# Twelve late turns, an earlier first step: reordering the middle stage of a two-layer gated cross-attention kernel

## The chip, the cores and the metric

One Trainium2 (trn2) chip, one of its cores. The metric is the device time of one execution in microseconds (us), median of the timed runs. The engines of the core are named as the profile names them: PE (TensorE, matrix products), PEld (its weight loads), DVE (VectorE), ACT (ScalarE), POOL (GpSimd) and SP (SyncE, which issues DMAs).

## The reference

Two layers over `x` of 4 batches x 512 rows x 512 columns, with a context of 4 x 512 x 256:

```python
# layer 0, per batch: attention over the context's 512 rows, which mixes the 512 columns of x
query, key = ctx @ Wq.T + bq, ctx @ Wk.T + bk                      # 512 x 128
attention = softmax(query @ key.T)                                 # 512 x 512
x = x + tanh(g_xattn[0]) * (layernorm(x) @ attention.T)
weight = einsum('oin,n->oi', sigmoid(pweight) - sigmoid(nweight), exps * sigmoid(mask)) * scale
x = x + tanh(g_ffn[0]) * (layernorm(x) @ weight.T + bias)          # bias from 4 bits as well
# layer 1: cross-attention, 16 heads of 128, then 16 experts of which each row takes 4
q, k, v = rmsnorm(layernorm(x) @ Wq), rmsnorm(ctx @ Wk), ctx @ Wv
x = x + tanh(g_xattn[1]) * (softmax(q @ k.T / sqrt(128)) @ v @ Wo)
x = x + tanh(g_ffn[1]) * experts(layernorm(x), topk_idx, topk_weight)
```

What matters below: layer 1's queries need a normalised and transposed copy of `x` for every batch, and the experts need a routing table that is made from `topk_idx` alone. In this problem only batch 0 goes through the experts.

## The kernel before, in words

**Numbers in two parts.** Every product of two fp32 matrices is made of three PE products (`product`): each operand is held as a rounded high part and the low rest, and `lo*hi`, `hi*hi`, `hi*lo` are summed in one PSUM bank. The high part is a copy on ACT (`copy_hi`, L824), the low one a subtraction on DVE (`lower`, L1153) or POOL (L1661).

**Stage 0 (layer 0).** Each engine runs a list of two-character entries written by hand: `L0_ORDER` for PE, `ACT_ORDER`, `DVE_ORDER`, `POOL_ORDER`, and `LOAD_ORDER` for SP. The letters: `K` splits of the context and of Wq/Wk, `Q` the two small projections of batch b, `R` the bias turned into a row, `S` and `T` the energies and the softmax, `P` the turned probabilities, `G` and `W` the sixteen bit planes and the four slices of the weight made of them, `C0` to `C15` the sixteen row tiles of the first wide product (attention times x), `E0` to `E15` those of the second (normalised x times weight, 12 products of 512 columns each), `m`/`C`/`E` on POOL the layer norms, `d` and `D` the normalised rows of batch b (ACT) and their turns (PE transposes, ACT high, DVE low), `B` the bias added. `f` and `F` are the same as `d` and `D` after the second wide product: they make `xnT`, the operand of layer 1's queries, for batches 0 to 3. A turn is four transposes of 128x128 into one PSUM bank. `Y` and `Z` on DVE work out the bit weights and the bias.

**Stage 1 (layer 1's attention) and the experts.** `step(t)` runs for t = 0 to 65. A step is a software pipeline three deep: the projections of item t (`key_value`, `query`), the scores and probabilities of item u = t-1, the values and output product of item w = t-2. Items 0 to 15 are the 16 heads of batch 0; the items from 16 on are, head by head, batches 1, 2 and 3. From step 20 the experts' work is packed in beside it. Before, steps 0 and 1 stand at the end of the hand-written lists: `X0` is step 0 (`key_value`, `ranks`, `query`), `x0` its key turn on PE, `X1` step 1. The routing table runs inside them: `experts()` and `slots()` (DVE) and `ranks()` (PE) in step 0, `places()` (DVE `x0`) after it, `tokens_in`, `spot` (DVE) and `table()` (PE) in step 1.

**What ties step 0 to stage 0.** `ranks` writes both `w_bank`s, which the wide products use, so it waits for the last of them. The high and low parts of layer 0's weight (`wf`) live in the tensors `kv` that hold keys and values of a step, so no step's keys can be written before E15. A step's scores wait for `q_lo` and `kT_lo`, both made by DVE in its own list order:

```python
if i == 0:
    need(pe, q_lo, 1, u, 1)
    need(pe, kT_lo, 1, u, 1)
```

Of the kernel before, what the change touches and what calls it, by code (L numbers as in the profile page):

```python
# [12 lines left out]
P = 128  # L13
# [29 lines left out]
def stages(text):  # L43
# [16 lines left out]
    E0 E1 E2 E3 D2 E4 E5 E6 E7 D3 E8 E9 F1 E10 E11 F0 E12 E13 F2 E14 E15 X0 x0 F3 X1""")  # L60
ACT_ORDER = stages("""
    K0 K1 K2 Q0 G0 R0 K3 S0 T0 A0 Q1 A1 P0 A2 A3 S1 K4 A4 A5 G1 T1 P1 K5 A6 Q2 A7 G2 d0 A8 G3 S2 A9 G4 W0 G5 A10 T2
    G6 G7 P2 Q3 A11 A12 A13 G8 W1 d1 G9 G10 S3 D0 G11 T3 G12 W2 P3 G13 A14 G14 G15 A15 W3 D1 d2 D2 d3 D3 f1 F1 f0 F0
    H0 f2 F2 X0 f3 x0 F3 z0 X1""")
DVE_ORDER = stages("""
    Y0 K0 K1 K2 Z0 Q0 R0 S0 G0 T0 m0 Q1 P0 S1 m1 C0 C1 T1 C2 C3 P1 G1 Q2 m2 G2 S2 C4 G3 C5 T2 G4 C6 G5 C7 G6 P2 G7
    Q3 m3 G8 C8 S3 G9 C9 G10 T3 G11 D0 P3 G12 C10 G13 C11 G14 C12 G15 C13 C14 C15 E0 E1 D1 E2 E3 D2 E4 E5 E6 E7 D3
    E8 E9 F1 E10 E11 F0 E12 E13 F2 E14 E15 X0 F3 x0 X1""")
POOL_ORDER = stages("""
    G0 K3 A0 A1 A2 m0 K4 A3 A4 m1 A5 G1 C0 G2 K5 A6 m2 G3 A7 G4 W0 A8 G5 A9 G6 A10 G7 C1 G8 W1 G9 A11 G10 A12 G11  # L70
    A13 G12 W2 G13 A14 G14 m3 G15 A15 W3 C2 B0 B1 C3 B2 E0 B3 E1 E2 H0 E3 X0 X1""")

LOAD_ORDER = stages("""
    c0 c1 g0 c2 x0 t0 x1 c3 t1 g1 c4 g2 x2 g3 t2 g4 g5 g6 g7 g8 t3 g9 x3 g10 g11 g12 g13 g14 g15""")
# [16 lines left out]
EARLY_TURNS, _ = numbered("DFPR", L0_ORDER[:L0_ORDER.index(("X", 0))])  # L91
EARLY = max(n + (1 if key[0] == "R" else NT) for key, n in EARLY_TURNS.items())
# [10 lines left out]
P_BANK = (1, 0, 1, 1)  # L103
LAST_SCORES = NI
# [19 lines left out]
def flamingo_kernel(nc, x, xT, ctxT, vecs, w0, bits, w1, w_gu, w_dn, topk_idx, topk_w, x0_dram, rows_dram, y_dram, out):  # L124
# [3 lines left out]
    with ExitStack() as ctx:  # L128
# [117 lines left out]
        def turn_bank(n):  # L246

            return (t_bank + j_bank)[n % 4] if n < EARLY else (s_bank + t_bank[1:] + j_bank[:1])[(n - EARLY) % 4]

# [4 lines left out]
        def prob_bank(t, i):  # L254

            return (t_bank[1], t_bank[0], s_bank[1], j_bank[1])[i] if t == LAST_SCORES else t_bank[P_BANK[i]]

# [8 lines left out]
        def energy_bank(b, i):  # L266
# [40 lines left out]
            sem("s_mm"), sem("s_max"), sem("p_exp"), sem("p_turned"), sem("p_hi"), sem("p_lo"))  # L307
        pv_mm, o_hi, o_lo, w_mm, w_added = sem("pv_mm"), sem("o_hi"), sem("o_lo"), sem("w_mm"), sem("w_added")
# [52 lines left out]
        def _(sp):  # L361
# [12 lines left out]
            sp.dma_start(vec[:], vecs).then_inc(vec_in, 16)  # L374
            sp.dma_start(split_stage[0], w0).then_inc(split_in[0], 16)
            for kind, b in LOAD_ORDER:
                if kind == "c":
                    context(b)
                elif kind == "x":
# [105 lines left out]
        def _(pe):  # L485
# [7 lines left out]
            def turn(n, tile, ready, count):  # L493
# [3 lines left out]
                wait(pe, turned_lo, n - 3 if n < EARLY or n - 4 >= EARLY else 0)  # L497
                if n == EARLY + 3:
                    pe.wait_ge(kv_second, 1)
# [3 lines left out]

            pe.wait_ge(ident_ready, 2)
            def turn_keys(t):
                need(pe, k_scaled, 1, t, 1)
                if t:
                    need(pe, p_lo, 4, t - 1, 2)
# [4 lines left out]
            def step(t):  # L513
# [19 lines left out]
                def probs(i):  # L533
# [4 lines left out]
                    if i == 1:  # L538
                        need(pe, q_ss_out, 1, u, 1)
                    elif t != LAST_SCORES:  # L540
# [26 lines left out]
                def project_out(i):  # L567
                    if not value:
                        return
                    if t == LAST_VALUES and i == 2:  # L570
                        need(pe, o_lo, 1, w, 2)
                    if i == 0:
# [55 lines left out]
                def ranks():  # L628
                    pe.wait_ge(expert_ready, 1)
                    pe.wait_ge(wide_added, 2 * NT * B)  # L630
                    oh = expert_of.rearrange("p c e -> p (c e)")
                    pe.matmul(w_bank[0][:, 0:PAIRS * E], before, oh, start=True, stop=False)
                    for c in range(PAIRS - 1):
                        last = pe.matmul(
                            w_bank[0][:, (c + 1) * E:PAIRS * E].rearrange("p (c e) -> p c e", e=E), every,
                            expert_of[:, c:c + 1, :].to_broadcast([P, PAIRS - 1 - c, E]), start=False,
                            stop=c == PAIRS - 2)
                    last.then_inc(ranks_mm, 1)
                    pe.matmul(w_bank[1][:, 0:PAIRS * E], every, oh, start=True, stop=True).then_inc(ranks_mm, 1)

                def table():
                    pe.wait_ge(place_ready, 1 + NT)
                    for c in range(PAIRS):
# [61 lines left out]

                if t == LAST_SCORES:
# [29 lines left out]
                values()  # L736
                key_value(0)
# [4 lines left out]
                if t == 0:  # L742
                    ranks()
                project_out(0)
                scores(3)
# [20 lines left out]
                if t == 1:  # L766
                    table()

            pe.wait_ge(const_ready, 2)
            for kind, b in L0_ORDER:  # L770
# [8 lines left out]
                elif kind == "Q":  # L779
# [3 lines left out]
                    for cj, n in ((0, 0), (0, 1), (1, 0), (1, 1)) if b == 0 else ((0, 0), (1, 0), (0, 1), (1, 1)):  # L783
                        if b == 0 and n == 0:
                            pe.wait_ge(split_lo, 2 + cj)
                        at = (n * CT + cj) * P
# [11 lines left out]
                elif kind in "CE":  # L798
# [12 lines left out]
                    last.then_inc(wide_mm, 1)  # L811
                elif kind == "X":
                    pe.wait_ge(turned_lo, EARLY if b == 0 else TURNS)
                    step(b)
                elif kind == "x":
                    turn_keys(b)
# [4 lines left out]
        def _(act):  # L821
# [4 lines left out]
            def turned_tile(kind, b, i, n):  # L826
# [4 lines left out]
            act.wait_ge(vec_in, 16)  # L831
            nc.scalar.activation(tanh_g[:], vec[:, G_X:G_X + 4], ACT.Tanh).then_inc(gates_tanh, 1)
            nc.scalar.activation(small[:, 0:NBITS], vec[:, MASK:MASK + NBITS], ACT.Tanh, scale=0.5).then_inc(
                mask_tanh, 1)
# [17 lines left out]
            def step(t):  # L852
# [21 lines left out]
                def values_hi():  # L874
# [3 lines left out]
                    need(act, w_mm, 4, w - 1, 4)  # L878
                    copy_hi(oT[0][:], j_bank[0][:]).then_inc(o_hi, 1)
# [114 lines left out]
                def key_query_parts():  # L994
                    query_hi()
                    key_hi()

                if t == 0:
                    return key_parts, key_query_parts, query_squares
# [11 lines left out]
                if t == LAST_VALUES:  # L1011
                    last_values_hi(0)
                    last_values_hi(1)
                    return
                if fresh(t):
# [19 lines left out]
                else:  # L1035
# [5 lines left out]
                    if t and fresh(t):  # L1041
# [5 lines left out]
                    softmax(2)  # L1047
                    softmax(3)
# [14 lines left out]
            act.wait_ge(gain_ready, 1)  # L1063
            for kind, b in ACT_ORDER:
                if kind == "H":
# [13 lines left out]
                elif kind == "Q":  # L1079
                    for n, bias in enumerate((BQ, BK)):  # L1080
# [46 lines left out]
                elif kind == "X":  # L1127
                    if b == 0:
                        act.wait_ge(bias_added, NT * B)
                        act.wait_ge(wf_lo, DT)  # L1130
                        step(0)[0]()
                    else:
                        step(b)
                elif kind == "x":
                    step(0)[1]()
                elif kind == "z":
                    step(0)[2]()
# [765 lines left out]
```

## Time and profile before

| | us |
|---|---|
| median of 3 runs | 1476.35 (1474.93 to 1476.39) |
| the profiled execution, its own time | 1475.46 |
| its span in the trace | 1473.7 |
| PE busy / share of the span | 1439.3 / 98% |
| DVE busy / share | 1104.9 / 75% |
| ACT busy / share | 977.4 / 66% |
| POOL busy / share | 862.7 / 59% |

The profile is one execution. Its span is 1.8 us shorter than its own time and 2.65 us shorter than the median. Times of rows count from the start of the span. A busy share is an average over stages: whether an engine is the limit of a stage is read from what the other engines wait for there. In a row of the timeline the bracket gives the idle time of the engine just before the instruction, and what ended it.

### The profile page before, as it was taken

The numbers are of one execution on the slowest core, as the hardware profiler recorded it, in microseconds if no ns is written. First come the engines' busy times: TensorE is split into PE (matmuls) and PEld (weight loads), VectorE is DVE, ScalarE is ACT, GpSimd is POOL, SyncE is SP. The second block draws the span as 40 slices with busy tenths as digits, with TensorE's granted clock in tenths as the row PEclk, the third lists the DMA queues.
The fourth block names the chain that finished last, engine by engine and source line by source line (L and its number), as shares of the span: only waits on it lengthen the run. The fifth ranks groups of instructions, "written<-read, shape, count | busy, mean of one in ns | idle before, by whom it ended". The sixth has DMA issues, their size and how long they took to land.

```text
span 1473.7 us, 23708 instructions
## 1 busy us (share of the span) xinstructions
PE 1439.3 (98%) x8070; PEld 1224.9 (83%) x8070; DVE 1104.9 (75%) x2100; ACT 977.4 (66%) x2224; POOL 862.7 (59%) x701
## 2 busy tenths in 40 slices
PE   6999899999999999999999999999999999999998
PEld 5778788888888888888888888888888888888887
DVE  6887776777767877767777777777777777788777
ACT  6874566666776677676766767676766766666664
POOL 4775355555554575666666657575756655664441
PEclk9999999999999999999999999999999999999999
DMA  8420011111111334433343433344343341321002
GB/s 322 143 79 1 23 46 48 44 44 51 44 37 65 119 104 144 135 123 127 129 145 109 146 126 131 120 138 136 115 135 126 123 136 43 101 87 37 8 0 87
DMA packets 55495, 142.74 MB, mean 97 GB/s; under 512 B 5392, under 2 KB 5392, under 8 KB 55376
## 3 DMA queue, kind: packets, MB, share of 16 engines
q1 hardware_dynamic: 51616, 128.90, 25.7%
q0 software_dynamic: 3760, 12.32, 2.9%
q8 instruction: 66, 1.08, 0.3%
q14 instruction: 53, 0.43, 0.1%
HBM read 126.79 MB, written 14.42 MB: 96 GB/s over the span
## 4 chain that ended last, share of the span: by engine, by line
PE 81%; DVE 7%; POOL 4%; ACT 4%; issue 2%; DMA 0%; ACTq 0%; SPq 0%; DVEq 0%; POOLq 0%
PE w_bank L489 10%; PE w_bank L491 10%; PE w_bank L490 10%; PE j_bank L489 9%; PE j_bank L491 9%; PE j_bank L490 9%; PE t_bank L543 7%; PE s_bank L489 4%; PE s_bank L491 4%; PE s_bank L490 4%; PE t_bank L510 2%; POOL q_scale L1701 2%; POOL wo_lo L1661 2%; ACT prob L863 1%; DVE q_ss L1302 1%
## 5 line engine op out<-in xcount | busy, mean ns | idle before, releaser
L863 ACT ACTIVATE prob<-s_bank,neg_bias,q_scale 128x512 f32<-128x512 f32 x255 | 197.7, 776 | 205.8 <-DVE neg_bias L1310 205.8
L1153 DVE TENSOR_TENSOR probT_lo<-t_bank,probT_hi 128x512 fp32r<-128x512 f32 x262 | 177.5, 688 | 176.1 <-ACT probT_hi L824 176.1
L1364 DVE SCALAR_TENSOR_TENSOR x_sb<-w_bank,inv_sum,x_sb 128x512 f32<-128x512 f32 x254 | 188.2, 743 | 0.0
L1289 DVE TENSOR_REDUCE neg_max<-s_bank 128x1 f32<-128x512 f32 x255 | 168.3, 681 | 0.0
L1661 POOL TENSOR_TENSOR xnT_lo<-xnT_raw,xnT_hi 128x512 fp32r<-128x512 f32 (+2 forms) x47 | 126.3, 2687 | 60.8 <-ACT xnT_hi L824 60.8
L543 PE MATMUL t_bank<-ident,prob 128*128 128x128 f32 x1016 | 152.9, 273 | 3.1 <-ACT prob L863 3.0
L1701 POOL TENSOR_TENSOR q_scale<-q_ss,minus_half 128x4 f32<-128x4 f32 x64 | 65.8, 1028 | 152.4 <-DVE q_ss L1302 152.4
L824 ACT CAST probT_hi<-t_bank 128x512 fp32r<-128x512 f32 x262 | 151.1, 590 | 1.8 <-PE t_bank L501 1.8
L489 PE MATMUL j_bank<-wkv_lo,cT_hi 128*128 128x256 f32 x512 | 145.1, 283 | 0.6 <-DVE oT_lo L1153 0.3
L491 PE MATMUL j_bank<-wkv_hi,cT_lo 128*128 128x256 f32 x512 | 144.6, 282 | 0.0
L490 PE MATMUL j_bank<-wkv_hi,cT_hi 128*128 128x256 f32 x512 | 144.5, 282 | 0.0
L543 PEld LDWEIGHTS t_bank<-ident,prob 128*128 128x128 f32 x1016 | 121.8, 140 | 23.9 <-ACT prob L863 4.4
L1661 POOL TENSOR_TENSOR sqs_lo<-xn,sqs_hi 128x512 fp32r<-128x512 f32 x62 | 80.3, 1295 | 100.8 <-ACT xn L941 100.8
L1661 POOL TENSOR_TENSOR cT_round<-cT_raw,x_round 128x1408 fp32r<-128x1408 f32 (+1 forms) x31 | 104.4, 3369 | 59.1 <-ACT x_round L824 59.1
L489 PE MATMUL w_bank<-wo_lo,oT_hi 128*128 128x512 f32 x254 | 112.9, 444 | 2.6 <-POOL wo_lo L1661 0.9
L489 PE MATMUL s_bank<-kv_lo,qT_hi 128*128 128x512 f32 x255 | 109.8, 430 | 4.8 <-DVE xnT_lo L1153 4.8
L824 ACT CAST oT_hi<-j_bank 128x512 fp32r<-128x512 f32 x64 | 36.9, 577 | 113.7 <-PE j_bank L491 113.7
L489 PE MATMUL j_bank<-xnT_lo,wq_hi 128*128 128x512 f32 x256 | 108.5, 424 | 0.0
L489 PEld LDWEIGHTS j_bank<-wkv_lo,cT_hi 128*128 128x128 f32 x512 | 97.3, 190 | 9.0 <-DVE oT_lo L1153 3.4
L490 PEld LDWEIGHTS j_bank<-wkv_hi,cT_hi 128*128 128x128 f32 x512 | 97.4, 190 | 4.6
L491 PE MATMUL j_bank<-xnT_hi,wq_lo 128*128 128x512 f32 x256 | 101.1, 395 | 0.0
L491 PE MATMUL s_bank<-kv_hi,qT_lo 128*128 128x512 f32 x255 | 100.8, 395 | 0.0
(297 smaller groups left out, 4446.2 us busy)
## 6 DMA issues: line engine op xcount, KB each, us to landing
stage<-w SPq DMA_DIRECT2D x96, 256.0 KB, 3.1
xnT_raw<-w_gu SPq DMA_DIRECT2D x31, 704.0 KB, 5.4
cT_raw<-w_gu SPq DMA_DIRECT2D x31, 704.0 KB, 4.8
xnT_raw<-w_dn SPq DMA_DIRECT2D x16, 768.0 KB, 4.3
cT_raw<-w_dn SPq DMA_DIRECT2D x15, 768.0 KB, 4.8
planes<-bits SPq DMA_DIRECT2D x16, 512.0 KB, 4.2
y<-stage SPq DMA_DIRECT2D x31, 256.0 KB, 4.2
x_sb<-x SPq DMA_DIRECT2D x5, 1024.0 KB, 10.8
```

The costliest lines, as they stand in the source:

```text
L489: pe.matmul(dst, lh, rl, start=first, stop=False)
L490: pe.matmul(dst, lh, rh, start=False, stop=False)
L491: return pe.matmul(dst, ll, rh, start=False, stop=last)
L510: last = pe.transpose(t_bank[0][:, j * P:(j + 1) * P], kv_raw[:, j, 0:HD], ident[:])
L543: last = pe.transpose(prob_bank(t, i)[:, j * P:(j + 1) * P], prob[:, i, j * P:(j + 1) * P], ident[:])
L824: return nc.scalar.copy(dst, src)
L863: nc.scalar.activation(prob[:, i, :], score_bank(t, i)[:], ACT.Exp, bias=neg_bias[:, u % 2, i:i + 1], scale=q_scale[:, u % 2, i:i + 1], ac ...
L1153: return nc.vector.tensor_tensor(dst, src, hi, ALU.subtract)
L1289: nc.vector.tensor_reduce(neg_max[:, u % 2, i:i + 1], score_bank(t, i)[:], AX_X, ALU.max, negate=True).then_inc(own_max, 1)
L1364: nc.vector.scalar_tensor_tensor(out=here, in0=w_bank[0][:] if packed else out_bank(t, i)[:], scalar=inv_sum[:, w % 2, i:i + 1], in1=here, ...
L1661: return nc.gpsimd.tensor_tensor(dst, src, hi, ALU.subtract)
L1701: nc.gpsimd.tensor_tensor(q_scale[:, u % 2, :], q_ss[:, u % 2, :], minus_half[:], ALU.pow).then_inc(q_scale_ready, 1)
```

## The change

Six edits.

1. **Twelve late turns.** `F1`, `F2`, `F3` (with `f1` to `f3`) leave the lists. Steps 4 to 15 each take one row tile of batches 1 to 3: `late_norm` (ACT) at the head of the step, `late_turn` (PE, four transposes into `w_bank[1]`) after `project_out(0)`, `late_copy` (ACT) between `softmax(2)` and `softmax(3)`, `late_lower` (DVE) after `shift(3)`. `project_out(1)` waits for it.
2. **Step 0 among the wide products.** Its keys and values (PE `k0`) stand before E12, its query and key turn (`q0`, `x0`) before E14. `key_hi` and what follows it wait for E15.
3. **Routing among the wide products.** `experts` is DVE's `a0` after E5, `ranks` PE's `r0` after E9 and in the `s_bank`s, `slots` in three parts `b0` to `b2` around E10 to E12, `places` before E13. `table()` goes from the end of step 1 to step 2, after `values()`; the first `values_hi` waits for it, two of the four `spot`s come at the end of step 1.
4. **Step 1 with an order of its own** on PE, ACT and DVE, and its third bank for turned probabilities in the `w_bank`s. The weights of step 1 are split at the end of step 0.
5. **First loads.** SP issues `w0`, `c0` and then `vec`; `gain`, the two tanh and the bit weights move behind the first splits; the first projection starts with the product that needs high parts alone.
6. **Idle turns.** Sixteen transposes of the identity into an unused bank as PE's first work.

```diff
-    E0 E1 E2 E3 D2 E4 E5 E6 E7 D3 E8 E9 F1 E10 E11 F0 E12 E13 F2 E14 E15 X0 x0 F3 X1""")
+    E0 E1 E2 E3 D2 E4 E5 E6 E7 D3 E8 E9 r0 F0 E10 E11 k0 E12 E13
+    q0 x0 E14 E15 X1""")
 ACT_ORDER = stages("""
-    K0 K1 K2 Q0 G0 R0 K3 S0 ... W3 D1 d2 D2 d3 D3 f1 F1 f0 F0
-    H0 f2 F2 X0 f3 x0 F3 z0 X1""")
+    K0 K1 v0 K2 Q0 G0 R0 K3 S0 ... W3 D1 d2 D2 H0 d3 D3 f0 F0
+    k0 q0 z0 x0 X1""")
 DVE_ORDER = stages("""
-    Y0 K0 K1 K2 Z0 Q0 R0 S0 ... E4 E5 E6 E7 D3
-    E8 E9 F1 E10 E11 F0 E12 E13 F2 E14 E15 X0 F3 x0 X1""")
+    K0 K1 Y0 K2 Z0 Q0 R0 S0 ... E4 E5 a0 E6 E7 D3
+    E8 E9 F0 b0 E10 b1 E11 b2 E12 x0 E13 q0 E14 E15 k0 M0 X1""")
 POOL_ORDER = stages("""
-    ... W3 C2 B0 B1 C3 B2 E0 B3 E1 E2 H0 E3 X0 X1""")
+    ... W3 C2 B0 B1 C3 I0 B2 E0 B3 H0 E1 E2 k0 w0 q0 v0 E3 X1""")
 LOAD_ORDER = stages("""
-    c0 c1 g0 c2 x0 t0 ...
+    c0 v0 c1 g0 c2 x0 t0 ...
...
+LATE = {4 + n: key for n, key in enumerate((b, i) for b in range(1, B) for i in range(NT))}
+LATE_HEAD = min(LATE)
+WARM = 16
...
 PE:
+                if t == 1:
+                    key_value(0)
+                    scores(0)
+                    scores(1)
+                    query_squares()
+                    key_value(1)
+                    query(range(DT))
+                    probs(0)
+                    scores(2)
+                    scores(3)
+                    probs(1)
+                    key_turn()
+                    probs(2)
+                    probs(3)
+                    return
...
                 values()
+                if t == 2:
+                    table()
                 key_value(0)
...
                 project_out(0)
+                late_turn()
                 scores(3)
...
+                def late_turn():
+                    if t not in LATE:
+                        return
+                    pe.wait_ge(late_normed, t - LATE_HEAD + 1)
+                    need(pe, w_added, 4, w, 0)
+                    for j in range(DT):
+                        last = pe.transpose(w_bank[1][:, j * P:(j + 1) * P], late_row(t)[:, j * P:(j + 1) * P], ident[:])
+                    last.then_inc(late_turned, 1)
...
+            for n in range(WARM):
+                pe.transpose(t_bank[1][:, n % 4 * P:(n % 4 + 1) * P], ident[:], ident[:])
...
 ACT:
+                late_norm()
                 if fresh(t):
                     split_wkv(t)
...
                     softmax(2)
+                    late_copy()
                     softmax(3)
...
+                elif kind == "x":
+                    act.wait_ge(wide_mm, 2 * NT * B)
+                    step(0)[3]()
...
 DVE:
                     add(0)
                     maximum(3)
                     shift(3)
+                    late_lower()
...
+                if t == 1:
+                    squares_out()
+                    maximum(0)
+                    maximum(1)
+                    shift(0)
+                    shift(1)
+                    tokens_in()
+                    spot(0)
+                    spot(1)
+                    maximum(2)
+                    shift(2)
+                    maximum(3)
+                    shift(3)
+                    probs_lo(0)
+                    values_rows()
+                    query_lo()
+                    key_lo()
+                    probs_lo(1)
+                    probs_lo(2)
+                    probs_lo(3)
+                    spot(2)
+                    spot(3)
+                    return
```

## Rows read from the trace of the kernel before

**Rows 1.** Two stretches: length; busy PE, PEld, DVE, ACT, POOL; granted clock; DMA share, GB/s
```profile
170.00:210.00 40.00, 33.52 (x187) 27.93 (x188) 28.43 (x58) 24.00 (x61) 20.21 (x19) 0.96 0.10 33
210.00:1473.00 1263.00, 1255.30 (x7152) 1073.87 (x7151) 943.85 (x1777) 843.00 (x1967) 739.03 (x566) 1.00 0.29 96
```

**Rows 2.** PE's timeline, 136 to 166 us: start, duration, instruction
```profile
136.56 0.60 PE L501 MATMUL t_bank<-ident,xn 128*128 128x128 f32 x4
...
138.22 0.47 PE L489 MATMUL w_bank<-kv_lo,xnT_hi 128*128 128x512 f32 x1
...
158.24 0.28 PE L489 MATMUL j_bank<-wkv_lo,cT_hi 128*128 128x256 f32 x1
...
161.19 0.39 PE L632 MATMUL w_bank<-wo_lo 128*128 128x256 f32 x1
...
163.22 0.40 PE L489 MATMUL j_bank<-xnT_lo,wq_hi 128*128 128x512 f32 x1
...
165.95 0.60 PE L510 MATMUL t_bank<-ident,kv_raw 128*128 128x128 f32 x4
```

**Rows 3.** PE's timeline, 168 to 201 us
```profile
173.13 0.80 PE L489 MATMUL s_bank<-kv_lo,qT_hi 128*128 128x512 f32 x1 [4.83 <-DVE xnT_lo L1153]
...
176.28 0.43 PE L626 MATMUL t_bank<-sqs_lo,ones 128*128 128x512 f32 x1
...
180.53 0.66 PE L543 MATMUL t_bank<-ident,prob 128*128 128x128 f32 x4 [2.38 <-ACT prob L863]
...
193.28 0.40 PE L489 MATMUL j_bank<-probT_lo,kv_hi 128*128 128x512 f32 x1
...
200.32 0.50 PE L489 MATMUL w_bank<-wo_lo,oT_hi 128*128 128x512 f32 x1 [0.15 <-POOL wo_lo L1661]
```

**Rows 4.** DVE's timeline, 163 to 170 us
```profile
163.42 0.42 DVE L1229 TENSOR_REDUCE h_row<-w_bank 128x16 f32<-128x256 f32 x1 [1.00 <-PE w_bank L639]
...
164.79 1.26 DVE L1235 TENSOR_TENSOR stage<-stage 128x256 f32<-128x256 f32 x1
...
169.34 0.69 DVE L1153 TENSOR_TENSOR qT_lo<-j_bank,qT_hi 128x512 fp32r<-128x512 f32 x1
```

**Rows 5.** The page's groups of instructions: the high-part copies on ACT
```profile
L824 ACT CAST probT_hi<-t_bank 128x512 fp32r<-128x512 f32 x262 | 151.1, 590 | 1.8 <-PE t_bank L501 1.8
```

**Rows 6.** Timeline of all engines, 0 to 15 us
```profile
1.19 0.42 SPq L375 DMA_DIRECT2D kv_raw<-w  x1
...
5.05 0.62 ACT L824 CAST cT_hi<-stage 128x512 fp32r<-128x512 f32 x1 [0.45 <-DMA stage<-ctxT]
...
6.54 0.77 PE L489 MATMUL s_bank<-cT_lo,oT_hi 128*128 128x512 f32 x1 [6.54 <-DVE cT_lo L1153]
...
7.36 0.17 DVE L1197 TENSOR_TENSOR bias_col<-vec 128x16 f32<-128x16 f32 x1
...
9.74 0.43 DVE L1210 COPY kv_raw<-bias_col 128x512 f32<-128x512 f32 x1
...
12.76 0.75 DVE L1598 SCALAR_TENSOR_TENSOR qT_lo<-s_bank,vec,qT_hi 128x512 fp32r<-128x512 f32 x1 [0.53 <-ACT qT_hi L1083]
...
13.56 0.49 PE L489 MATMUL s_bank<-qT_lo,qT_hi 128*128 128x512 f32 x1 [0.82 <-DVE qT_lo L1598]
```

**Rows 7.** Busy time and granted clock, 25 to 35 us, columns as in the first group
```profile
25.00:30.00 5.00, 4.26 (x13) 3.12 (x12) 4.75 (x10) 4.23 (x10) 3.15 (x6) 0.62 1.05 387
30.00:35.00 5.00, 5.00 (x17) 3.93 (x17) 2.67 (x8) 2.57 (x4) 4.35 (x3) 0.70 0.82 293
```

**Rows 8.** A settled step: timelines of ACT, DVE and PE, 280 to 300 us
```profile
282.34 0.78 ACT L863 ACTIVATE prob<-s_bank,neg_bias,q_scale 128x512 f32<-128x512 f32 x1 [3.99 <-DVE neg_bias L1310]
...
291.28 1.29 DVE L1153 TENSOR_TENSOR probT_lo<-t_bank,probT_hi 128x512 fp32r<-128x512 f32 x2 [1.41 <-ACT probT_hi L824]
...
283.52 0.60 PE L543 MATMUL t_bank<-ident,prob 128*128 128x128 f32 x4
...
284.19 0.39 PE L490 MATMUL s_bank<-kv_hi,qT_hi 128*128 128x512 f32 x1
```

More of the change, by code:

```diff
@@ L502, in turn, with ranks @@
                 last.then_inc(turned, 1)
+            def ranks():
+                pe.wait_ge(expert_ready, 1)
+                oh = expert_of.rearrange("p c e -> p (c e)")
+                pe.matmul(s_bank[0][:, 0:PAIRS * E], before, oh, start=True, stop=False)
+                for c in range(PAIRS - 1):
+                    last = pe.matmul(
+                        s_bank[0][:, (c + 1) * E:PAIRS * E].rearrange("p (c e) -> p c e", e=E), every,
+                        expert_of[:, c:c + 1, :].to_broadcast([P, PAIRS - 1 - c, E]), start=False,
+                        stop=c == PAIRS - 2)
+                last.then_inc(ranks_mm, 1)
+                pe.matmul(s_bank[1][:, 0:PAIRS * E], every, oh, start=True, stop=True).then_inc(ranks_mm, 1)
             pe.wait_ge(ident_ready, 2)
@@ L626, in query_squares @@
                     pe.matmul(t_bank[0][:], every_row, sqs[1][:], start=False, stop=True).then_inc(q_ss_mm, 1)
[L628 to L639, printed above, removed]
                 def table():
                     pe.wait_ge(place_ready, 1 + NT)
+                    need(pe, p_lo, 4, 0, 4)
                     for c in range(PAIRS):
@@ L992, in key_parts, with query_parts, late_norm, late_copy @@
                     key_squares()
-                def key_query_parts():
+                    split_wkv(1)
+                def query_parts():
                     query_hi()
-                    key_hi()
+                    split_wq(1)
+                def late_norm():
+                    if t not in LATE:
+                        return
+                    b, i = LATE[t]
+                    act.wait_ge(shift_ready, SHIFT["E", b] + 1)
+                    act.wait_ge(blocks_ready, 1)
+                    wait(act, late_turned, t - LATE_HEAD - 1)
+                    nc.scalar.activation(late_row(t), x_sb[:, b, i, :], ACT.Identity, bias=ln_shift[:, b, i:i + 1],
+                                         scale=rstd[:, b, i:i + 1]).then_inc(late_normed, 1)
+                def late_copy():
+                    if t not in LATE:
+                        return
+                    act.wait_ge(late_turned, t - LATE_HEAD + 1)
+                    copy_hi(late_tile(0, t), w_bank[1][:].rearrange("p (j q) -> p j q", j=4)).then_inc(late_hi, 1)
                 if t == 0:
-                    return key_parts, key_query_parts, query_squares
+                    return key_parts, query_parts, query_squares, key_hi
                 if t == LAST_SCORES:
@@ L1014, in step @@
                     return
+                if t == 1:
+                    first_rows()
+                    second_rows()
+                    key_squares()
+                    softmax(0)
+                    softmax(1)
+                    query_hi()
+                    probs_hi(0)
+                    softmax(2)
+                    key_hi()
+                    softmax(3)
+                    query_squares()
+                    probs_hi(1)
+                    probs_hi(2)
+                    probs_hi(3)
+                    return
+                late_norm()
                 if fresh(t):
@@ L1762, in squares_lo @@
                     lower(sqs[1][:], squares(t), f32(sqs[0][:])).then_inc(sq_lo, 1)
-                if t and fresh(t):
+                if t == 0:
+                    return scale_keys, squares_lo, values_lo
+                if t > 1 and fresh(t):
                     lower_wkv(t)
```

198 lines of the change are left out of this document (131 added, 67 removed).

## The prediction

> **What bounds the kernel now.** I read the page first (PE 98% busy), then busy time by stretch. From 210 us to the end PE is busy 1255.3 of 1263 us at full clock [rows 1]: there the time is what PE has to do, and an edit counts by the PE work it adds or takes. From 170 to 210 us PE is busy 33.5 of 40 us, at a mean granted clock of 0.96. So the idle lies in stage 0's first 100 us and at the seam, steps 0 and 1. PE's timeline of the seam shows three things: E10 to X0 run without a hole [rows 2]; then PE stands 4.83 us for DVE's last `xnT_lo` and 2.38 us for the first softmax [rows 3]. DVE's own timeline says why: the nine instructions of `slots` fill 163.42 to 169.34 and the query's low part, the keys' low part and four `F3` tiles queue behind them [rows 4]. After the 4.83 us the first products take 0.43 us each instead of 0.23 (eight and a bit of them fill 173.13 to 176.5): that is 1.2 GHz in place of 2.4.
>
> **The seam before.** From the end of E9 (136.56) to step 2's first output product (200.32) pass 63.76 us [rows 2, 3]. I rebuild this stretch.
>
> *PE work of the new order, without waits.* A block of turns, F1, takes 138.22 - 136.56 = 1.66 us. E10 to E15 take 158.24 - 136.56 - 3 x 1.66 = 16.70, so a product of 512 columns takes 16.70 / 72 = 0.232. Step 0's keys and values 2.95, `ranks` 2.03, a query 2.73 [rows 2]. One turn inside a step costs 0.44: 283.52 to 284.19 holds a turn and one product of 0.23 [rows 8]. Up to step 1: 16.70 + F0 1.66 + 2.03 + 2.95 + 2.73 + key turn 0.44 = 26.51. Step 1: 2.95 + 2.73 + four scores of three products 2.78 + squares 0.46 + five turns 2.20 = 11.12. Step 2's first two scores and squares: eight products, 1.86. From its values to its first output product 7.04 as before (193.28 to 200.32, 0.15 idle in it [rows 3]), and `table` now inside it: 16 transposes' worth, 4 x 0.44 = 1.76. Sum 48.29.
>
> *What hides the moved work.* `experts` after E5 and `slots` around E10 to E12 cost nothing: an E tile takes PE 2.78 us and the next but one needs DVE's add. If the cover goes, E12 is late next. `key_hi` waits for E15, then `key_lo`: about 0.7 each, beside step 1's first `key_value` half of 1.48. First score about level, 0.1 lost. `values_lo` (POOL) and `E3` stand before step 1's query scale; `first_rows` on ACT waits for `values_lo`, and `softmax` waits behind it. The squares' chain took 4.25 us before (176.28 to 180.53 [rows 3]); PE now has half a `key_value` and a whole query over it, 1.48 + 2.73 = 4.21. Nothing lost to speak of.
>
> *Where I expect waits.* From step 1's first turn on PE has only five turns, two scores and step 2's opening: 5 x 0.44 + 2 x 0.70 + 1.86 = 5.5, before `values`, which need all four low parts. ACT has three softmaxes of 0.78 [rows 8] and about 0.1 for each sum, eight copies or squares at some 0.55 [rows 5], 7.0 in all, and DVE's last low part 0.7: with hand-overs 8.0. Minus 5.5 makes 2.5 us of waits, in several pieces, too short for the clock to fall. With the 0.1: 2.6. Bounds: nothing lost, or all the idle of the old seam again, 4.83 + 2.38 = 7.2. I take 2.6, since the 4.83 had a known cause (`slots` and F3 ahead of `qT_lo`) that is gone.
>
> Seam after: 48.29 + 2.6 = 50.9, so 12.9 us less. Part of it is PE work only moved: F1 to F3.
>
> **The twelve late turns.** 12 x 0.44 = 5.3 us on PE, on its bound stretch, so in full. The rest lies beside it: ACT stands 3.99 us before `softmax(0)`, and `late_norm` (about 0.75) fits; `late_copy` falls between two softmaxes, where ACT waits for the shift; DVE stands 1.41 us before `probs_lo(1)`, and `late_lower` is 0.69 [rows 8, 4]. Queued behind it: `probs_lo(1)`, and `project_out(1)` on PE, with a score, two turns and a whole query between, 4.3 us after the late turn. POOL's weight splits come 0.75 us later because `split_wkv` stands behind `late_norm`. Bounds: 0.415 a turn as in F1, 5.0 in all; or 0.44 and 0.7 of uncovered DVE each, 13.7. I take 5.3.
>
> Net of the seam: 12.9 - 5.3 = 7.6 us.
>
> **First loads and idle turns.** `w0` and `c0` are issued 0.45 us earlier (`vec` no longer ahead of them; 1.19 was `w0`'s issue). PE can begin on high parts when ACT's copy of `c0` is done, 5.05 + 0.62 - 0.45 = 5.2, instead of 6.54. But `S0` waits for DVE's `qT_lo`, and DVE has its own queue: `c0`'s low part done near 5.95, then gain and bit weights (five small instructions, about 1.1), `c1`'s low part 0.7, then the bias columns, 7.36 to 10.17 before, 2.8 us [rows 6], so 10.55; then two `qT_lo` of 0.75: 12.05 in place of 13.5. The gain is 1.5 us, whether the first twelve products take 0.43 or 0.23 us. The sixteen idle turns, at some 0.22 us each even at 1.2 GHz (twice a quarter of 0.44), run from about 1.5, when the identity is written, to 5.0, before there is anything to do. Does 1.5 us survive to the seam? In the timelines of the four engines no wait between 12 and 105 us ends on a DMA, so the chain should shift as a whole. Bounds: 0 (a DMA, saturated at a share of 1.05 until past 30 us, becomes late [rows 7]) and 1.5 plus what the clock gives.
>
> The clock: 25 to 35 us runs at 0.62 and 0.70 of full [rows 7], that is 3.8 and 3.0 us at 1.2 GHz, half of which is lost: 3.4 at most. The mean over 170 to 210 us is 0.96 [rows 1]. The Trainium skill (TensorE: Matmul & The Clock Gate, Part 1) says that the throttled state is the default and that activity releases it; the slow first products after 4.83 us of idle agree. By that rule the idle turns would bring Q0 to the full clock, 2.4 us sooner on PE, which DVE's queue hides as said, and the clock may be lost again before S0.
>
> **Sum.** 7.6 + 1.5 = 9.1 us. The profiled execution took 1475.46 with a span of 1473.7; its span would be 1464.6. The median of the runs shown, 1476.35, lies 0.9 above that execution; minus 9.1 it gives 1467.2, the prediction.
>
> **Rivals.**
>
> *A. DVE stretched by POOL beside the wide products.* `slots`' fourth instruction took 1.26 us, its like 0.42, while POOL was at `step(0)`'s keys [rows 4]. The new places put nine of `slots` and the rest of `places` beside POOL's weight splits and `scale_keys`. The Trainium skill (GPSIMD Engine Reference, Specifications) says that the two engines share their SBUF interfaces; the row agrees, and that is against the change. If all fifteen take 0.85 more, DVE has 12.8 us more to do in the 26.5 us, on top of about 22: 8 us over, of which, spread over tiles, I would see 3 to 6 on PE. Then 1470 to 1473. Against it: in the row only two of nine were long.
>
> *B. The clock.* With PE's gaps moved, the stretch at 25 to 35 us may stay at 2.4 GHz: 3.4 us more gained, 1464; with the second such stretch too, 1462. Against it: its cause, PE's gaps while DVE and ACT work on S0 and P0, is unchanged.
>
> *C. Late turns make steps wait (slower).* `project_out(1)` waits for `late_lo`, which stands behind DVE's `shift(3)`; ACT's `softmax(3)` waits behind `late_copy`. If the hand-over PE, ACT, DVE came back to PE late in every step, twelve steps lose. To eat 9.1 us each must lose 0.76; at 1.25 it is 15 us lost, 1482. It turns slower by more than 0.2% from 1.0 us a step (12.1 lost, 1479.3). For it: DVE has only 1.41 us there. Against it: `late_copy` starts when the turn ends, and PE has scores, a turn, half a query, another turn and half a query before `project_out(1)`.
>
> *D. No gain in front.* Something else, `c1` or DVE, holds S0 at 13.5: 1468.7.
>
> **How the numbers follow.** A difference of 0.2% (3 us) is about what this kernel's measurement tells from none. The forecast with D, 1464.5 to 1470: 0.64. A, 1470 to 1474: 0.15, of which 0.03 lies within 0.2%. B, 1461 to 1464.5: 0.15. C: 0.04. Seam waits at their upper bound, 4.6 more, with a part of A: 0.02, no change. That gives faster 0.91, same 0.05, slower 0.04. The range that leaves out no more than 0.2: 1462 to 1471.5.
>
> **What the profile would show.** Right: PE without a hole from E8 to step 1; `ranks` before F0; step 1's first score within 0.3 us of its first `key_value`; 2 to 3 us idle in pieces before step 2's values; steps 4 to 15 longer by 0.44 each, step 16 as before; S0's first product near 12.05. Wrong: `w_bank` products among E10 to E15 idle on DVE `x_sb` (A); the granted clock at 1.00 from 25 to 35 us (B); PE waiting in steps 4 to 15 on `late_lo` or a softmax (C); S0 at 13.5 (D).

## The result and the profile after

| | before | after |
|---|---|---|
| median of the comparison, us | 1476.37 (1474.93 to 1476.85) | 1463.55 (1463.31 to 1464.93) |
| profiled execution, us | 1475.46 | 1463.32 |
| its span, us | 1473.7 | 1461.5 |
| mean granted clock | 0.995 | 0.998 |

The ratio is 0.9916, 95% interval 0.9904 to 0.9928: 12.8 us faster where 9.1 were forecast, within the range. A second comparison gave 1462.44 against 1476.59, ratio 0.9905 (0.989 to 0.992).

Stretches of the changed kernel, columns as in [rows 1]:

```profile
10.00:15.00 5.00, 4.09 (x13) 3.14 (x14) 3.01 (x6) 2.48 (x5) 3.64 (x2) 0.66 1.06 399
25.00:30.00 5.00, 4.82 (x21) 4.00 (x22) 4.75 (x13) 4.25 (x9) 3.69 (x6) 1.00 1.05 387
30.00:35.00 5.00, 5.00 (x24) 4.14 (x23) 3.65 (x9) 2.62 (x6) 4.92 (x5) 1.00 0.81 278
50.00:55.00 5.00, 3.84 (x11) 3.10 (x12) 3.42 (x5) 3.02 (x8) 4.74 (x7) 0.72 0.41 152
...
160.00:200.00 40.00, 38.07 (x212) 30.81 (x213) 31.34 (x64) 25.59 (x65) 22.23 (x23) 1.00 0.10 27
200.00:1461.00 1261.00, 1253.21 (x7163) 1072.90 (x7162) 946.10 (x1774) 853.98 (x1984) 737.78 (x564) 1.00 0.29 96
```

The seam is now busy 38.07 of 40 us at full clock, against 33.52 at 0.96 [rows 1]. And 25 to 35 us, at 0.62 and 0.70 before [rows 7], runs at 1.00; low clock shows at 10 to 15 and from 50 on instead (0.94 from 55 to 60). (These figures are means over 5 us. Read in windows of 1 us, a low stretch stands at 0.50, which is 1.2 of 2.4 GHz, with other values only at its ends.)

PE's timeline of the changed kernel, its first 12 us and then the seam:

```profile
5.19 0.50 PE L840 MATMUL s_bank<-cT_hi,oT_hi 128*128 128x512 f32 x1 [0.30 <-ACT cT_hi L892]
...
11.57 0.79 PE L505 MATMUL s_bank<-qT_lo,qT_hi 128*128 128x512 f32 x1 [0.66 <-DVE qT_lo L1736]
...
132.10 0.28 PE L521 MATMUL s_bank<-wo_lo 128*128 128x256 f32 x1
...
134.02 0.60 PE L515 MATMUL t_bank<-ident,xn 128*128 128x128 f32 x4
...
158.22 0.28 PE L505 MATMUL j_bank<-wkv_lo,cT_hi 128*128 128x256 f32 x1
...
160.04 0.47 PE L505 MATMUL s_bank<-kv_lo,qT_hi 128*128 128x512 f32 x1 [0.23 <-DVE kv_lo L1496]
...
168.91 0.66 PE L538 MATMUL t_bank<-ident,kv_raw 128*128 128x128 f32 x4
169.66 0.66 PE L573 MATMUL w_bank<-ident,prob 128*128 128x128 f32 x4
171.11 0.66 PE L573 MATMUL t_bank<-ident,prob 128*128 128x128 f32 x4 [0.80 <-ACT prob L927]
...
173.63 0.49 PE L657 MATMUL t_bank<-sqs_hi,ones 128*128 128x512 f32 x1 [0.16 <-POOL sqs_lo L1815]
...
174.65 0.50 PE L505 MATMUL j_bank<-probT_lo,kv_hi 128*128 128x512 f32 x1 [0.29 <-DVE probT_lo L1262]
...
183.42 0.50 PE L505 MATMUL w_bank<-wo_lo,oT_hi 128*128 128x512 f32 x1
```

From the end of E9 (132.10, where `ranks` begins) to step 2's first output product (183.42) pass 51.3 us, against 63.76: 12.4 less. The 4.83 and 2.38 us of idle [rows 3] are gone; what is left before step 2's values is 0.23, 0.80, 0.16 and 0.29, 1.5 us.

The sum of the two profiles has two marks, a tile of `x_sb` in stage 0 that waits for the same row of POOL in each kernel, and DVE's `q_ss` of step 2. Before:

```profile
99.21 0.75 DVE L1623 SCALAR_TENSOR_TENSOR x_sb<-w_bank,row_gain,x_sb 128x512 f32<-128x512 f32 x1 [0.96 <-POOL row_shift L1819]
...
194.21 0.69 DVE L1302 TENSOR_REDUCE q_ss<-xn 128x4 f32<-128x512 f32 x1
```

After:

```profile
94.64 0.75 DVE L1761 SCALAR_TENSOR_TENSOR x_sb<-w_bank,row_gain,x_sb 128x512 f32<-128x512 f32 x1 [0.97 <-POOL row_shift L1977]
...
177.31 0.69 DVE L1414 TENSOR_REDUCE q_ss<-xn 128x4 f32<-128x512 f32 x1
```

The tile comes 4.6 us earlier, `q_ss` 16.9 us. So the front brought 4.6 (forecast 1.5), the stretch between the marks 12.3 (95.0 to 82.7; forecast 12.9). The shift falls to 11.8 by step 16, 5.1 for the twelve late turns (forecast 5.3), and ends at 12.2, the difference of the spans. In this pair of profiles seam and late turns came out as forecast and the front did not; most of the runs look into it. The pair is one execution of each kernel, and the medians below divide the gain otherwise.

### The profile page after: what moved, and what is told of

It reads as the page before. It is cut to its first block, busy times and chain, and to the rows that moved or that the text cites. A ratio compares the mean times of both kernels' runs of the same rounds, so it can differ in the third digit from the quotient of the medians.

```text
span 1461.5 us, 23763 instructions
## 1 busy us (share of the span) xinstructions
PE 1437.8 (98%) x8086; PEld 1223.0 (84%) x8086; DVE 1107.0 (76%) x2100; ACT 977.5 (67%) x2224; POOL 864.5 (59%) x701
## 3 DMA queue, kind: packets, MB, share of 16 engines
q1 hardware_dynamic: 51616, 128.90, 26.1%
## 4 chain that ended last, share of the span: by engine, by line
PE 82%; DVE 7%; ACT 4%; POOL 4%; issue 2%; DMA 0%; ACTq 0%; SPq 0%; DVEq 0%; POOLq 0%
PE w_bank L505 10%; PE w_bank L507 10%; PE w_bank L506 10%; PE j_bank L505 9%; PE j_bank L507 9%; PE j_bank L506 9%; PE t_bank L573 7%; PE s_bank L505 4%; PE s_bank L507 4%; PE s_bank L506 4%; PE t_bank L538 2%; POOL q_scale L1855 2%; POOL wo_lo L1815 2%; ACT prob L927 1%; PE t_bank L657 1%
```

## Experiments

Each compares with runs of the kernel before on the same chip. Three numbers of each run's profile are worked out as above: the tile's time, from the tile to step 2's `q_ss`, and where the granted clock is below 1.00. Every execution also has a span and a mean clock of its own, but only one execution of each run has a profile.

| run | ratio (95%) | tile, us | tile to `q_ss` | clock below 1.00 at, us |
|---|---|---|---|---|
| before | 1 | 99.21 | 95.0 | 25-35, 55-65, 170-180 |
| changed | 0.9916 (.9904-.9928) | 94.64 | 82.7 | 10-15, 50-60 |
| changed, again | 0.9905 (.9890-.9920) | 96.76 | 82.6 | 10-20, 65-75 |
| no idle turns | 0.9937 (.9921-.9954) | 96.42 | 82.8 | 65-70, 85-90 |
| old loads | 0.9944 (.9928-.9961) | 99.44 | 82.8 | 20-30, 65-75, 85-95 |
| old front | 0.9934 (.9917-.9950) | 98.45 | 82.7 | 20-30, 65-75, 85-95 |
| before + idle turns | 0.9996 (.9986-1.0005) | 97.43 | 96.6 | 10-20, 65-75, 85-95, 165-180, 190-195 |
| late turns doubled | 0.9947 (.9934-.9961) | 93.57 | 82.6 | 50-55 |
| step 0 late | 0.9938 (.9924-.9951) | 97.41 | 87.8 | 20-30, 65-75, 85-95, 160-170 |
| routing late | 0.9941 (.9927-.9954) | 97.13 | 86.6 | 10-20, 65-75, 85-95, 170-180 |
| both late | 0.9965 (.9953-.9977) | 97.14 | 88.0 | 10-20, 65-70, 85-95, 160-170 |
| F1 in stage 0 | 0.9918 (.9905-.9932) | 94.13 | 84.6 | 50-60 |
| front filled | 0.9922 (.9908-.9935) | 96.49 | 82.7 | 65-75, 85-95 |
| all gaps filled | 0.9918 (.9904-.9931) | 94.96 | 82.6 | none |

**The front, edit by edit.** First the changed kernel without its idle turns.

```
-WARM = 16
+WARM = 0
```

> The changed kernel without the sixteen idle turns. Theory I (the idle turns decide at which clock the first wide product runs): the first projection runs at 0.43 us a product, S0 still starts near 11.6 to 12 since DVE's queue ends there, and the stretch at 1.2 GHz between 25 and 35 us is back: about 2.8 us lost, 1466.4. Theory P (the phase: the earlier start alone moved PE's gaps so that the stretch vanished): 25 to 35 us stays at a granted 1.00, S0 near 11.6 to 12, the time 1463.5 to 1464.

1465.66 against 1475.98. PE's first products, and the busy time and clock of the same stretch:

```profile
4.90 0.77 PE L840 MATMUL s_bank<-cT_hi,oT_hi 128*128 128x512 f32 x1 [4.90 <-ACT cT_hi L892]
5.46 0.63 PE L842 MATMUL s_bank<-cT_hi,oT_lo 128*128 128x512 f32 x1
5.89 0.63 PE L844 MATMUL s_bank<-cT_lo,oT_hi 128*128 128x512 f32 x1
...
7.97 0.39 PE L842 MATMUL s_bank<-cT_hi,oT_lo 128*128 128x512 f32 x1
8.20 0.39 PE L844 MATMUL s_bank<-cT_lo,oT_hi 128*128 128x512 f32 x1
...
5.00:10.00 5.00, 4.28 (x12) 3.08 (x12) 4.21 (x18) 1.93 (x4) 0.00 (x0) 1.00 0.96 320
```

Up to 7.6 us the products start 0.43 us apart, after that 0.23: the first six run at half speed. The clock column shows 1.00 there all the same, so in the first microseconds of a run it must be read beside the products, and the table's last column leaves out such a start (the kernel before has one too, its twelve products of Q0). With the idle turns they start 0.23 or 0.24 us apart wherever nothing else holds them (6.25, 6.49, 6.72). S0 starts at 11.49, with the idle turns at 11.57: with the new loads they do nothing for S0, as forecast. And 25 to 35 us runs at 1.00 here too, so it isn't the idle turns that keep that stretch.

Second, the idle turns kept, and the order of loads, splits and first products of before.

```
+            sp.dma_start(vec[:], vecs).then_inc(vec_in, 16)      (ahead of w0)
-    c0 v0 c1 g0 c2 x0 t0 ...
+    c0 c1 g0 c2 x0 t0 ...         (also: ACT v0, DVE Y0 ahead of K0; Q0 waits for split_lo first)
```

> The changed kernel with the first loads, the order of the first splits and the first products of before; the idle turns stay. S0 starts at 13.0 to 13.5 in place of 11.57: 1.5 to 2 us lost in any case. Theory I: the stretch between 25 and 35 us stays fast, so 1465.5. Theory P: it comes back, 2.8 us more, 1468.3.

1467.13, between the times of the two theories. S0 comes at 13.41. The run with step 0 late, described further down, has the changed front; its profile has the same three low stretches of stage 0 as this one, S0 at 11.68 and the tile at 97.41 against 99.44. That pair says 2.0 us, but part of it is one transfer: the first weights landed late in this execution. ACT's first copy here, and in the next run, which has the same loads:

```profile
5.32 0.62 ACT L882 CAST oT_hi<-kv_raw 128x512 fp32r<-128x512 f32 x1 [2.37 <-DMA kv_raw<-w]
```

```profile
3.96 0.62 ACT L882 CAST oT_hi<-kv_raw 128x512 fp32r<-128x512 f32 x1 [1.01 <-DMA kv_raw<-w]
```

The next run has low clock at the same places too, S0 at 12.41 and the tile at 98.45. Against it the changed front is worth 0.7 us at S0 and 1.0 at the tile.

Third, both edits undone; fourth, the idle turns alone put into the kernel before.

```
+            for n in range(16):
+                pe.transpose(t_bank[1][:, n % 4 * P:(n % 4 + 1) * P], ident[:], ident[:])
```

> The changed kernel with both front edits undone: first loads as before and no idle turns. What is left is the seam and the late turns. By the decomposition of the two traces (4.58 us of the gain are there at 100 us, 7.6 come later) the stretch between 25 and 35 us is slow as before and the time 1468.2 on both theories. If it came out at 1466 or less, the front edits had not made the 4.58.

> The kernel before with the sixteen idle turns alone. Theory I: the first projection runs at 0.23 us a product, S0 starts 1 to 2 us earlier (its second qT_lo waits for PE there), and the stretch between 25 and 35 us is fast: 3 to 4.5 us gained, 1472 to 1473.4. Theory P: S0 is 1 to 2 us earlier and the stretch is as it falls; if slow, 1474.5 to 1475.5.

They took 1465.74 and 1474.85. The first is under the 1466 that the expectation had named: the edits of the front had not made the 4.6. With both undone the kernel is still 10.2 us faster than before, so of the 12.8 the front's edits are worth some 3, seam and late turns some 10, each of them with an uncertainty of 2 to 3 us. The edits of the front don't add either: the ratio is 0.9934 with neither, 0.9937 with the loads alone, 0.9944 with the idle turns alone and 0.9916 or 0.9905 with both. The values with both lie just outside the intervals of the other three, and the intervals themselves touch: a gain of both together is likely, one of either alone is not seen.

The two profiles with the old front say 8.4 (spans 1473.7 and 1465.3): most executions of before are slower than the profiled one (mean clock 0.993 or 0.994, profiled 0.995), and the seam of before varies too, 95.0 and 96.6 in its two profiles, the longer one with low clock at 165 to 180 and at 190. The seam without idle has no such stretch to lose. Idle turns alone: no difference (0.9996); 25 to 35 us is at full clock, and 65 and 85 pay instead. The low stretches move, and none of the four edits decides them. But in this last run S0 starts at 12.01, 1.5 earlier than in the kernel before, whose Q0 ran at half speed to its end:

```profile
12.01 0.49 PE L489 MATMUL s_bank<-qT_lo,qT_hi 128*128 128x512 f32 x1 [0.66 <-DVE qT_lo L1600]
```

With the old loads, then, the idle turns can bring S0 forward. But the old front, with neither edit, had S0 at 12.41: seven of its first twelve products ran at half speed, in the kernel before all twelve. So 1.15 of the 2.0 us that S0 gained in the first pair of profiles (13.56 to 11.57) also come and go with the execution.

**The changed kernel again.** No edit.

> The changed kernel once more, unedited, for a second profile and a time beside the edits of the same call. If the places where TensorE's clock falls belong to the kernel (its gaps, in time), the second profile shows the same two stretches, at 10 to 15 and 50 to 60 us, and a span within 0.3 of 1461.5. If they depend on the execution, a stretch moves or one comes or goes, and the span moves with it by 1 to 2 us while the seam (the shift of the query squares against an x_sb tile of stage 0) stays within 0.1. The ratio to the kernel before should lie in 0.990 to 0.993.

The profiled execution had a span of 1464.5, 3.0 more than the first, with the same stretch between the marks (82.6) and the tile 2.1 later. The other three spans were 1460.4, 1460.6 and 1460.7, at a mean clock of 0.999. So one kernel takes 1460.4 to 1464.5. In the two profiled executions 2.1 of the 3.0 us arise in stage 0. The other 0.9 arise near 495 us, where the experts' first rows arrive later in the second execution (second row) than in the first:

```profile
491.57 0.63 PE L676 MATMUL w_bank<-ident,x_sb 128*128 128x128 f32 x4 [0.49 <-DVE x_sb L1476]
```

```profile
494.98 0.66 PE L676 MATMUL w_bank<-ident,x_sb 128*128 128x128 f32 x4 [1.77 <-DMA x_sb<-rows,slot_token]
```

One place in stage 0 where the two executions part, in DVE's and POOL's timelines. The first execution:

```profile
61.42 0.72 DVE L1788 SCALAR_TENSOR_TENSOR kv_raw<-stage,bit_w,kv_raw 128x512 f32<-128x512 f32 x1
...
61.51 1.78 POOL L1994 TENSOR_TENSOR stage<-stage 128x512 f32<-128x512 f32 x1 [0.30 <-ACT stage L1222]
...
65.82 0.63 PE L515 MATMUL t_bank<-ident,xn 128*128 128x128 f32 x4 [1.49 <-DVE probT_lo L1262]
```

The second:

```profile
61.00 1.29 POOL L1994 TENSOR_TENSOR stage<-stage 128x512 f32<-128x512 f32 x1
...
61.15 1.69 DVE L1788 SCALAR_TENSOR_TENSOR kv_raw<-stage,bit_w,kv_raw 128x512 f32<-128x512 f32 x1
...
66.62 0.63 PE L515 MATMUL t_bank<-ident,xn 128*128 128x128 f32 x4 [2.99 <-DVE probT_lo L1262]
```

In the first DVE starts 0.09 us ahead of POOL: DVE takes 0.72 and POOL 1.78. In the second POOL is ahead: POOL takes 1.29 and DVE 1.69. DVE's queue carries the 1 us on to the low part that PE's next turn waits for, and PE's gap is 3.0 instead of 1.5 us. All fourteen profiles fall into these two kinds: 0.72 in the four that have low clock at 50 to 60 (before, changed, late turns doubled, F1 in stage 0), 1.67 to 1.69 in the ten that don't. The Trainium skill (GPSIMD Engine Reference, Specifications) says that the two engines share their SBUF interfaces, with contention for DVE instructions that have two SBUF inputs. This instruction has two; the rows agree.

**A late turn's price.** The four transposes twice:

```
-                    for j in range(DT):
+                    for j in range(2 * DT):
+                        j = j % DT
```

> Each late turn issues its four transposes twice into the same bank. If the twelve steps are bound by TensorE, the second four cost what the first four cost, 0.43 less what a transpose in a row saves: 0.35 to 0.43 a step, 4.2 to 5.2 us in all over the unedited changed kernel. Rival, that a late turn is paid through a wait (its copy on ScalarE or its low part on VectorE, late by the same time): more than 0.6 a step, over 7 us. Rival, that the late turns stand in slack: under 1 us.

PE's turn in step 4, changed kernel and then this one:

```profile
218.76 0.60 PE L732 MATMUL w_bank<-ident,xn 128*128 128x128 f32 x4
219.12 0.48 PE L505 MATMUL s_bank<-kv_lo,qT_hi 128*128 128x512 f32 x1
```

```profile
217.66 1.04 PE L733 MATMUL w_bank<-ident,xn 128*128 128x128 f32 x8
218.46 0.47 PE L505 MATMUL s_bank<-kv_lo,qT_hi 128*128 128x512 f32 x1
```

No wait before or behind, and from step 2's `q_ss` to the last of the run 1270.5 instead of 1265.4: 5.1 more, 0.42 for each of the twelve steps (expected: 4.2 to 5.2 in all). The median lies 5.75 over the changed kernel's of the same comparison. Late turns are paid on PE alone.

**Step 0 and routing, each back behind E15, then both.** Their places in PE's order (DVE's likewise):

```
 changed:       E8 E9 r0 F0 E10 E11 k0 E12 E13 q0 x0 E14 E15 X1
 step 0 late:   E8 E9 r0 F0 E10 E11 E12 E13 E14 E15 k0 q0 x0 X1
 routing late:  E8 E9 F0 E10 E11 k0 E12 E13 q0 x0 E14 E15 r0 X1
 both late:     E8 E9 F0 E10 E11 E12 E13 E14 E15 k0 q0 x0 r0 X1
```

With routing late the ranks also go back to the `w_bank`s, and PE's second turn of probabilities in step 1 waits for `slots`; no row of PE waits there.

> Step 0's keys, query and key turn go back behind E15; routing stays among the wide products and the late turns stay. My theory (the seam's 4.83 us was VectorE's routing) expects little: the wait of the first score on key_lo is less covered, 0.5 to 3 us over the unedited changed kernel. Rival, that step 0 among the wide products is what carries the seam: 6 us or more.

> The ranks go back behind E15 into the w banks, and all fourteen instructions of slots and places behind step 0's keys on VectorE, ahead of the query squares' sums of step 1; step 0 stays among the wide products. My theory: VectorE is 3.8 + 3.9 us late at the first shift, of which step 1's query and key_value cover little more than now: 5 to 8 us over the unedited changed kernel, as idle time of TensorE before step 1's first turns. Rival, that step 0's place carries the seam: under 2 us.

> Step 0 and routing both go back behind E15; the first loads, the idle turns and the twelve late turns stay. Alone they cost 5.1 us (step 0) and 3.9 us (routing) in the stretch from the x_sb tile near 95 us to step 2's query squares, which took 82.6 us in the changed kernel. If the two causes add, the stretch takes 91.6. Of the 12.3 us that the change took out of it, 3 x 1.66 = 5.0 are the turns F1 to F3 moved elsewhere, so 7.3 are left for these two: if that account is whole, the stretch takes 89.9, and the median lies 7.3 us over the changed kernel's ratio. Rival, that they cover each other (routing's instructions lie beside step 0's waits): 87 to 88, no more than the larger one alone.

Between the marks they took 5.1, 3.9 and 5.4 us more than the changed kernel; the medians of the first two lie 4.5 and 5.7 over it in the same comparison, and with both the ratio is 0.9965. The profile with step 0 late is of its slowest execution (1470.89, median 1466.96). PE in it:

```profile
162.47 0.66 PE L538 MATMUL t_bank<-ident,kv_raw 128*128 128x128 f32 x4 [1.82 <-POOL kv_raw L1902]
...
163.69 0.58 PE L505 MATMUL j_bank<-wkv_lo,cT_hi 128*128 128x256 f32 x1 [0.57 <-POOL wkv_lo L1815]
```

With routing late, DVE from the first to the last of its fifteen instructions, and then PE:

```profile
162.12 0.42 DVE L1341 TENSOR_REDUCE h_row<-w_bank 128x16 f32<-128x256 f32 x1 [0.46 <-PE w_bank L529]
...
167.15 0.69 DVE L1365 TENSOR_TENSOR prob<-h_row,stage 128x512 f32<-128x512 f32 x1
...
171.61 0.66 PE L574 MATMUL t_bank<-ident,prob 128*128 128x128 f32 x4 [2.02 <-ACT prob L929]
```

My theory that step 0's place is worth little fell: without E12 to E15 over it, POOL's key scaling and the split of the next weights stand open, 2.4 us of PE, and a low clock follows (0.81 and 0.51 from 160 to 170). Routing takes 5.7 us of DVE there; of the forecast 5 to 8 the median gives 5.7, the profile 3.9. In the profiles the two cover each other: 5.4 together, the rival's answer. The medians say so only in part. With both late the ratio lies 0.0049 and 0.0060 over the changed kernel's two, 7 to 9 us with an uncertainty of some 2: less than the 10.2 of the two added, more than the larger alone, and about the 7.3 of the other account. The profiles alone don't decide between the two. By them, of the 12.3 us 5.0 are the turns F1 to F3 moved away and 5.4 these two, with low clock in the seam of all three late profiles. The last 1.9 I put to no experiment: step 1's own order of scores, squares and turns is all the change there that stays in these runs.

**F1 in stage 0.** Batch 1 turned behind E10, eight late turns left.

```
-LATE = {... for b in range(1, B) ...}
+LATE = {... for b in range(2, B) ...}
-    E8 E9 r0 F0 E10 E11 k0
+    E8 E9 r0 F0 E10 F1 E11 k0     (ACT: f1 F1 behind F0; DVE: F1 behind E10)
```

> Batch 1 is turned in stage 0 again, four turns behind E10, and only batches 2 and 3 in steps 4 to 11. By TensorE's work 1.66 us go back into the stretch before step 0 and four times 0.43 leave the steps: no difference, within 0.3 us of the sum. If late turning is itself worth something (ScalarE's eight and VectorE's four instructions pushed out of the wide products), it is 1 to 3 us slower than the changed kernel, as waits between E10 and step 1's query squares.

Ratio 0.9918, median 1462.78: level with the changed kernel. Between the marks 2.0 more, in the steps 1.8 less. Whether batch 1 is turned late or early makes no difference that these runs show.

**Filling PE's gaps.**

```
+ 12 idle turns behind Q0, 4 behind R0, 14 ahead of S1                    (front filled)
+ 14 ahead of C6, 12 ahead of D0, 12 ahead of P3, into drained banks      (all gaps filled, as well)
```

> Thirty more idle turns, in TensorE's waits of the first 25 us: 12 behind Q0, 4 behind R0, 14 ahead of S1, all into a bank that nothing holds. If a gap of TensorE is what sets off a stretch of low clock behind it, the stretch at 10 to 20 or 20 to 30 us, seen in four of the five profiles of this front so far, goes, the tile near 35 us comes at 34.3 as in the profile that lacked it, and the time falls by about 1 us. Rival, that the stretches come at their own times: one still begins between 10 and 30 us and the time is the same.

> The front's idle turns as in the fill of the first 25 us, and 38 more in the three later gaps of stage 0: 14 ahead of C6 (gap of 2.1 us near 50), 12 ahead of D0 (1.5 to 3.0 us near 65), 12 ahead of P3 (2.15 us near 85), each into a bank that is drained by then. If gaps of TensorE set the low stretches off, none is left in stage 0, the x_sb tile that came at 93.6 to 97.4 us comes at 93 or before, and the median lies 1 to 3 us under the changed kernel's, near 1460.5. Rival, that they come with the chip's own power and not with the gaps: stretches remain and the median is the changed kernel's, 1462 to 1464. Rival, that the fillers are in the way: slower by 0.5 to 1.5 us with the clock at 1.00.

With the front filled no low clock is left before 50 us, the tile near 35 us comes at 34.58 (late turns doubled 34.26, step 0 late 35.51), but stretches follow at 65 and 85: 1464.88. With all gaps filled the granted clock is 1.00 in each 5 us of the first 210 and 1.000 in the mean of all five executions. Here two of its windows, and behind them the same of the changed kernel's second profile:

```profile
65.00:70.00 5.00, 3.81 (x23) 3.06 (x24) 5.00 (x9) 5.00 (x9) 2.73 (x5) 1.00 0.30 106
85.00:90.00 5.00, 4.57 (x31) 3.25 (x31) 4.97 (x9) 4.93 (x8) 3.97 (x4) 1.00 0.00 0
```

```profile
65.00:70.00 5.00, 3.38 (x17) 3.07 (x18) 5.00 (x8) 5.00 (x10) 2.73 (x6) 0.75 0.36 113
85.00:90.00 5.00, 3.82 (x26) 2.78 (x27) 5.00 (x9) 4.98 (x8) 2.52 (x2) 1.00 0.07 15
```

Its spans are 1461.2 to 1461.8, a spread of 0.6, but the median is 1463.46. It isn't the 1460.5 hoped for: with PE's gaps filled the low stretches are gone, in five executions of five, yet in this profile as in the nine others without one near 50 us DVE's instruction falls under POOL's (1.67 us), and the tile comes at 94.96, not at 93.57. The expectation's last rival, that the idle turns are in the way, is not ruled out: the tile near 35 us came 0.3 later with the front filled than in the profile with late turns doubled, which has no low stretch there either. No version here beats the changed kernel by more than can be measured.

## Why the prediction came out

- *The seam, 12.9 less.* Right: 12.4. Up to step 1 I had 26.51 and PE took 26.1; from step 1 to step 2's values 12.98 of work and 2.6 of waits, 15.6, measured 16.4, of it 1.5 waits that the trace names. The turns of step 1 follow each other at 0.66 and 0.75 instead of 0.44. The rest, 8.8, as forecast. Part of the agreement is luck: the first stretch came 0.4 short, the second 0.8 long. And it holds for the pair of profiles. By the medians with the old front, seam less late turns brought 10.2 and not 7.6, because most executions of the kernel before are slower than the profiled one. The reason I gave for DVE's share, routing ahead of `qT_lo`, holds in part only: that step 0's place matters as much was not in my account. I had called waits of 2.5 us in pieces "too short for the clock to fall"; in stage 0, gaps of 1.5 to 2.3 us were followed by 1.2 GHz in some profiles and not in others.
- *Cover.* Step 1's first score 0.23 late; `ranks` ahead of F0; E10 to E15 without a wait on PE.
- *Late turns, 5.3.* Right: 5.1, on PE and nowhere else (rival C fell).
- *First loads, 1.5.* S0 came at 11.57, my 12.05 being 0.5 late. The mis-sized term of the sum is the front's, "The gain is 1.5 us": 4.6 in the pair of profiles, some 3 by the medians, 1.0 to 2.0 in profiles with equal low stretches. By the medians the 3.7 us that the change gained beyond the 9.1 are some 1 of front and 2.6 of seam, and neither is larger than the uncertainty. The sentence "whether the first twelve products take 0.43 or 0.23 us" holds for the new loads (11.49 and 11.57) and not for the old ones: in the kernel before ACT waited 4.04 us for those products before `qT_hi`, and idle turns alone brought S0 from 13.56 to 12.01.
- *The clock.* "Its cause, PE's gaps while DVE and ACT work on S0 and P0, is unchanged" was nearly true, and the conclusion wrong: PE still stood 1.87 us ahead of batch 1's energies (2.25 before), and no low clock followed in this profile. Two others of the same front show that it could have gone either way: PE stood 2.23 us there with step 0 late, and low clock followed (0.81 and 0.84 at 20 to 30), and 2.26 us with late turns doubled, and none did. Rival B's time, 1464, is what was measured, to 0.5; that is luck, since its mechanism holds for this pair of profiles and is not a property of the change. The Trainium skill's rule (TensorE: Matmul & The Clock Gate, Part 1), that the throttled state is the default and activity releases it, agrees with the run whose gaps are filled: 1.000 in five executions.
- *Rival A.* None of the nine `slots` instructions was long (0.39 to 0.43); one of `places` took 1.21 and no tile waited. The mechanism is real and sits elsewhere, at 61 us. *Rival D* fell: S0 came early.
- What stays open: why a gap of 1.5 to 2.3 us is followed by low clock in one execution and not in another, how the gain beyond the forecast divides between front and seam, and 1.9 us of the seam.

## What to carry to other kernels

Write the seam as a sum of PE work in the new order plus named waits: it came within 0.5 us. Small products of a single chain (first step, routing) are worth putting among wide products, but check each helper engine's queue there: POOL's scaling and the weight splits were 2.4 of the 5.1 us in the profile with step 0 late. For a term of a few us in a stretch with gaps, take a second profile of the same kernel first; here two executions differed by 3.0 us, as much as the edits of the front. And don't size an edit by a pair of profiles alone: a first transfer that landed 1.4 us late looked like the edit's own cost.

## What the hardware showed unasked

- Low clock that may save time: profiles with low clock at 50 to 60 us reach the `x_sb` tile at 93.57 and 94.13, the one with full clock throughout at 94.96, where DVE starts ahead of POOL at 61 us. I read it as a delay of ACT by the slower products (its exponent at 57.19 instead of 56.66 in the two profiles of the changed kernel, of which 0.3 us were there before, at 51) that also holds POOL back. This is not shown: no run tried it alone, and the profile at full clock has idle turns that the others lack.
- Two instructions of DVE and POOL that overlap: the one that starts second pays, 1.69 for 0.72 us (DVE), 1.78 for 1.29 (POOL), decided by 0.1 us of start.
- Each of the nine profiles whose PE gap ahead of D0's turns was 3.0 us had low clock right behind it; in the four with 1.5, and in the one where idle turns cut it to 1.7, none followed there.
